# Statistics of the edge messages: one instruction for two tiles, no aggregation, the sum of a small constant on GpSimd

## The chip, the core and the metric

The kernel runs on one core of one Trainium2 chip. The metric is the device time of one execution in microseconds (us). A core has TensorE (PE in the profile, with its weight loads as PEld), VectorE (DVE), ScalarE (ACT), GpSimd (POOL) and SyncE (SP). Each works through its own list of instructions in order; semaphores tie the lists together. An operation that a semaphore makes wait also holds everything behind it on the same engine.

## What is computed

One layer of a graph network over 3125 nodes of 256 features and 50000 edges, followed by a linear attention and a mixture of experts. The change is in the part that works on edges, cut here to that part:

```python
hi, hj = h[ei], h[ej]
msg = silu(concat(hi, hj, d2) @ mW1 + mb1)            # one row of 256 values an edge
mu  = mean(msg); var = mean(square(msg - mu))         # over the 256 values
msg = (msg - mu) * rsqrt(var + 1e-5) * ln_g + ln_b
msg = silu(msg @ mW2 + mb2)
agg = segment_sum(msg, ei)
```

## The kernel before

The edges are sorted by target node and cut into 224 units of 256 edges. A unit is two tiles (`G = 2`) of 128 edges, one edge a partition. The units run through a pipeline written out by hand: in step `n` each engine works on several units at different stages, in a fixed order. Ten steps make a turn (`TURN = 10`), because ten buffers are used in rotation; the first two turns and the tail are written out, and the turns between are a hardware loop.

What each engine does in step `n`:

- GpSimd works in pairs of units. `roots` waits for the variances of a pair (`spread_ok`) and computes 1/sqrt of four values a partition by a power of -0.5 (`nw_y`, L739). Then `gather` issues four indirect DMAs (L752), two for each of the two units that lie six units ahead, which bring rows of `dst_table` into `msg1`. Before two of the five pairs of a turn, `stage` copies the next gather indices (L747). All of this is one list in order.
- TensorE turns the normalised messages (`msg1n`, unit n-6, L832), multiplies unit n-7 by the second weight in three partial products (L1044, L1045, L1049), picks the source rows of unit n (L1061) and sums the messages of unit n-8 into their node rows (L1071).
- VectorE makes the one-hot rows of unit n+1 (L1700), on odd steps adds epsilon to the variances of a pair (`nw_v`, L1705), on even steps waits for GpSimd's root of the pair n-4 and forms the shift `1 - mean * root` of it (`nw_b`, L1712 and L1726), adds the node sums of unit n-9 (L1723), makes the low part of the split of unit n-6 (`msg1T_lo`, L1731), takes the statistics of both tiles of unit n-1 (L1738, twice), adds the picked and gathered rows of unit n (L1743), makes another one-hot (L1750), and aggregates the statistics of each tile into mean and variance (`emv`, L1755, twice).
- ScalarE evacuates the turned messages (L1331), normalises unit n-5 with `nw_y` as scale and `nw_b` as shift (L1338), and applies silu twice (L1345, L1350).

The number one in the shift carries the bias: the prepared second weight `w2c` has column sums that equal the bias of the product, so that a one added to every normalised value adds it. The statistics instruction gives six numbers for its input: count, mean and sum of squared deviations of the elements at even places, and the same of those at odd places. The aggregation merges these into one mean and one variance.

`roots` of pair m needs the variances of units m and m+1. VectorE waits for its result near the start of step m+4, ahead of L1723, L1731, L1738 and L1743 of that step.

## Time and profile before

| | us |
|---|---|
| device time, median of 3 runs | 1673.52 (1671.7 to 1680.5) |
| span of the profiled execution, first to last instruction | 1439.5 |
| median of the runs less that span | 234.0 |
| TensorE, VectorE, ScalarE, GpSimd busy, of the span | 1279.5, 1182.8, 932.1, 878.1 |
| edge pipeline, start of the first and of the last VectorE addition L1743 | 339.0 and 1052.4 |

The profiled execution's own device time is not recorded, only its span; the lowest and the median of the three timed runs are 0.1% apart. The edge pipeline is half of the span. A group row of the profile gives source line, engine, operation, tiles written and read, shapes and count, then busy time and the mean of one instruction. A row of the timeline gives the start, the time it took, the instruction, and in brackets the idle time of its engine before it and what ended it.

### The profile page before, as it was taken

To read this page: it belongs to the slowest core of one execution; us is meant where nothing else is said; L and a number is where in the kernel's file an instruction comes from. 1 tells how busy PE (TensorE), PEld (TensorE's weight loads), DVE (VectorE), ACT (ScalarE), POOL (GpSimd) and SP (SyncE) were. 2 spreads that over 40 slices of the span, in tenths; PEclk is the share of its full clock that TensorE was granted. 3 is DMA by queue.
4 is the path that set the end of the run, shared out by engine and by line. 5 is a ranking of instruction groups with operands and counts; after the bars stand their busy time and mean duration, and the time that the engine had idled before them with its cause. 6 is when DMAs were issued, how large, how long until landed. Compare 5 with 4: busy or idle time off the path is not lost.

```text
span 1439.5 us, 32698 instructions
## 1 busy us (share of the span) xinstructions
PE 1279.5 (89%) x8927; PEld 1149.6 (80%) x8928; DVE 1182.8 (82%) x3550; ACT 932.1 (65%) x1856; POOL 878.1 (61%) x885
## 2 busy tenths in 40 slices
PE   2678899996999999999999999999998847999990
PEld 1366778786999999999999999999886635988890
DVE  6999778726999999999999999999954688666662
ACT  0877444414778887888878888888753544666660
POOL 2188774035887778787777787878710014767761
PEclk7599999997999999999999999999999978999995
DMA  3911100022333333333333333336860162444447
GB/s 118 197 34 43 31 13 23 1 68 64 111 104 98 104 106 101 101 99 112 99 101 102 107 103 101 100 108 93 86 193 0 43 253 72 75 73 73 73 60 280
DMA packets 71387, 133.94 MB, mean 93 GB/s; under 512 B 23126, under 2 KB 43868, under 8 KB 70695
## 3 DMA queue, kind: packets, MB, share of 16 engines
q0 software_dynamic: 36560, 77.33, 24.1%
q1 hardware_dynamic: 33986, 52.62, 12.0%
q10 hardware_dynamic: 780, 3.24, 0.6%
q8 instruction: 31, 0.51, 0.2%
q14 instruction: 30, 0.25, 0.1%
HBM read 107.71 MB, written 25.29 MB: 92 GB/s over the span
## 4 chain that ended last, share of the span: by engine, by line
PE 71%; DVE 17%; DMA 4%; issue 3%; ACT 2%; POOL 1%; DVEq 0%; ACTq 0%; POOLq 0%; SPq 0%
PE ps L1071 12%; PE ps L832 9%; PE ps L1045 7%; PE ps L1049 7%; PE ps L1044 7%; PE ps L1061 7%; DVE place_val_t L1579 3%; DVE lane_hot_e_t L1574 2%; PE ps L1170 2%; PE ps L1201 2%; PE ps L1199 2%; PE ps L1200 2%; PE ps L1172 2%; PE ps L1171 2%; PE ps L1102 2%
## 5 line engine op out<-in xcount | busy, mean ns | idle before, releaser
L752 POOL DMA_INDIRECT msg_t<-dst_table,stage_idx x448 | 444.2, 991 | 128.7 <-issue 126.5
L1044 PE MATMUL ps<-w_hi_t,msg1T_hi_t 128*128 128x256 f32 x896 | 252.4, 303 | 0.0
L1338 ACT ACTIVATE msg1n_t<-msg_t,nw_b,nw_y 128x256 f32<-128x256 f32 x448 | 242.4, 590 | 0.0
L1350 ACT ACTIVATE msg_t<-msg_t 128x512 f32<-128x512 f32 x224 | 141.6, 632 | 149.4 <-DVE msg_t L1743 148.8
L1045 PE MATMUL ps<-w_lo_t,msg1T_hi_t 128*128 128x256 f32 x896 | 234.2, 283 | 0.0
L1071 PE MATMUL ps<-msg_t,hot_t 128*125 128x256 f32 x896 | 230.4, 379 | 0.2 <-issue 0.2
L1049 PE MATMUL ps<-w_hi_t,msg1T_lo_t 128*128 128x256 f32 x896 | 179.8, 282 | 0.0
L1045 PEld LDWEIGHTS ps<-w_lo_t,msg1T_hi_t 128*128 128x128 f32 x896 | 171.9, 192 | 0.0
L1044 PEld LDWEIGHTS ps<-w_hi_t,msg1T_hi_t 128*128 128x128 f32 x896 | 170.3, 190 | 0.0
L1738 DVE BATCH_NORM_STATS2 est<-msg_t 128x6 f32<-128x256 f32 x448 | 166.2, 413 | 1.2 <-ACT msg_t L1350 1.2
L1071 PEld LDWEIGHTS ps<-msg_t,hot_t 128*125 128x125 f32 x896 | 152.0, 187 | 14.2 <-issue 0.4
L1731 DVE TENSOR_TENSOR msg1T_lo_t<-ps,msg1T_hi_t 128x512 fp32r<-128x512 f32 x224 | 154.0, 688 | 2.7 <-ACT msg1T_hi_t L1331 2.5
L1743 DVE TENSOR_TENSOR msg_t<-ps,msg_t 128x512 f32<-128x512 f32 x224 | 151.2, 675 | 3.6 <-DMA msg_t<-dst_table,stage_idx 2.3
L721 POOL DMA_INDIRECT sorted_edges<-sort_sb_t,chunk_to x112 | 130.9, 1168 | 36.8 <-issue 33.8
L1049 PEld LDWEIGHTS ps<-w_hi_t,msg1T_lo_t 128*128 128x128 f32 x896 | 139.5, 191 | 0.0
L739 POOL TENSOR_TENSOR nw_y<-nw_v,minus_half 128x4 f32<-128x4 f32 x112 | 116.8, 1043 | 36.8 <-DVE nw_v L1705 29.6
L832 PE MATMUL ps<-ident,msg1n_t 128*128 128x128 f32 x896 | 135.7, 274 | 3.7 <-ACT msg1n_t L1338 3.7
L832 PEld LDWEIGHTS ps<-ident,msg1n_t 128*128 128x128 f32 x896 | 111.1, 140 | 29.1 <-ACT msg1n_t L1338 6.5
L1331 ACT ACTIVATE msg1T_hi_t<-ps 128x512 fp32r<-128x512 f32 x224 | 130.9, 584 | 3.5 <-PE ps L832 3.0
L1345 ACT ACTIVATE msg_t<-ps 128x512 f32<-128x512 f32 x224 | 129.9, 580 | 2.6 <-PE ps L1049 2.5
L1061 PE MATMUL ps<-src_hi_t,hotT_t 127*128 x448 | 120.0, 288 | 8.7 <-DVE hotT_t L1700 8.7
L1061 PE MATMUL ps<-src_lo_t,hotT_t 127*128 x448 | 119.5, 288 | 0.0
(374 smaller groups left out, 3081.1 us busy)
## 6 DMA issues: line engine op xcount, KB each, us to landing
near_rows<-row_list SPq DMA_DIRECT2D x44, 320.0 KB
w_sb_t<-in_L_ffn_W_dram SPq DMA_DIRECT2D x16, 512.0 KB, 8.5
msg_t<-dst_table,stage_idx POOLq DMA_INDIRECT x448, 2.8
res_t<-in_x_dram SPq DMA_DIRECT2D x1, 3125.0 KB
total<-zero_chunks_t SPq DMA_DIRECT2D x1, 3125.0 KB, 26.8
dst_table<-dst_stage SPq DMA_DIRECT2D x25, 125.0 KB
xm_table<-xm_t POOLq DMA_DIRECT2D x5, 625.0 KB, 7.5
sum_a_t<-total SPq DMA_DIRECT2D x5, 625.0 KB, 10.6
```

Source lines behind the costliest of these rows:

```text
L752: pool.indirect_dma_start(out=msg1[:, k, j, :], out_offset=None, in_=dst_table, in_offset=bass.IndirectOffsetOnAxis(stage_idx[:, G * k + j ...
L832: return pe.transpose(out_, in_, ident[0:rows, 0:rows])
L1044: pe.matmul(o[j], part(msg1T_hi, j, c), w2_hi[:, c, :], start=(c == 0), stop=False)
L1045: pe.matmul(o[j], part(msg1T_hi, j, c), w2_lo[:, c, :], start=False, stop=False)
L1049: m = pe.matmul(o[j], part(msg1T_lo, j, c), w2_hi[:, c, :], start=False, stop=(c == KD - 1))
L1061: m = pe.matmul(bank(1 + k % 2, D, first=j * D), hotT[0:HR, k, j * 128:j * 128 + 128], table[0:HR, bass.ts(blk[k], 1), :].rearrange("p a n ...
L1071: m = pe.matmul(bank(7 * (kl % 2), D, rows=NP), hot[:, kl % 2, j, 0:NP], msg2[:, kl % 2, j, :], start=(j == 0), stop=(j == G - 1))
L1338: m = A(msg1n[:, (kl + 1) % 2, j, :], msg1[:, kk, j, :], ACT.Identity, bias=nw_b[:, kk, j:j + 1], scale=nw_y[:, kk, j:j + 1])
L1350: A(v, v, ACT.Silu).then_inc(msg1_sb, 1)
L1731: dve.tensor_tensor(msg1T_lo[:, k % 2], bank(3 + k % 2), msg1T_hi[:, k % 2].bitcast(F32), ALU.subtract)\
L1738: st.did(dve.bn_stats(est[:, kk, j, :], msg1[:, kk, j, :]))
L1743: dve.tensor_tensor(v, bank(1 + k % 2), v, ALU.add).then_inc(pre_sb, 1)
```

## The change

- The two statistics instructions a unit become one over 512 elements. It reads the two tiles interleaved (`p j n -> p n j`), so that the elements at even places are tile 0 and those at odd places tile 1. Its six results are count, mean and sum of squared deviations of each tile.
- The aggregations (two a unit) are gone, and the buffer `emv` with them. The sum of squared deviations is 256 times the variance, so the root is now of `256 * var + 256 * eps`, which is the old root divided by 16. The second weight is multiplied by 16 instead, once, ahead of the pipeline.
- Epsilon is no longer added on VectorE (L1705 before) but on GpSimd: `roots` first adds `eps_sum` to the four sums, waits for that addition through a semaphore, and then takes the power. The statistics instruction itself now releases `spread_ok`, once a unit.
- The added one (divided by 16) is no longer added to the shift on VectorE (L1726 before) but in ScalarE's evacuation of the turned messages, as a bias, and in VectorE's low part, which becomes an operation with two arithmetic steps.

```diff
@@ roots, on GpSimd
-                pool.wait_ge(spread_ok, m // 2 + 1 if isinstance(m, int) else pairs + k // 2 + 1)
+                pool.wait_ge(spread_ok, m + 2)
                 if not isinstance(free, int) or free > 0:
                     pool.wait_ge(msg1n_sb, free)
+                st.did(pool.tensor_tensor(nw_v[:], est[:, k:k + 2, :, 2], eps_sum[:].rearrange("p (a b) -> p a b", b=G), ALU.add))
+                st.join()
                 pool.tensor_tensor(nw_y[:, k:k + 2, :], nw_v[:], minus_half[:].rearrange("p (a b) -> p a b", b=G),
                                    ALU.pow).then_inc(pow_ok, 1)
@@ edge_step, on ScalarE
-                    A(msg1T_hi[:, kl % 2], bank(3 + kl % 2), ACT.Copy).then_inc(msg1T_sb, 1)
+                    A(msg1T_hi[:, kl % 2], bank(3 + kl % 2), ACT.Copy, bias=1.0 / ROOT_D).then_inc(msg1T_sb, 1)
@@ edge_step, on VectorE
-                if k % 2 and here(n - 3, UNITS):
-                    slot = (k - 3) % TURN
-                    st.join()
-                    dve.tensor_scalar(nw_v[:], emv[:, slot:slot + 2, :, 1], EPS, None, ALU.add).then_inc(spread_ok, 1)
...
-                    nw.did(dve.scalar_tensor_tensor(shifts, emv[:, slot:slot + 2, :, 0], -1.0, nw_y[:, slot:slot + 2, :],
-                                                    ALU.mult, ALU.mult))
+                    dve.scalar_tensor_tensor(shifts, est[:, slot:slot + 2, :, 1], -1.0, nw_y[:, slot:slot + 2, :],
+                                             ALU.mult, ALU.mult).then_inc(rstd_ok, 1)
...
-                if pair_on:
-                    nw.join()
-                    dve.tensor_scalar(shifts, shifts, 1.0, None, ALU.add).then_inc(rstd_ok, 1)
...
-                    dve.tensor_tensor(msg1T_lo[:, k % 2], bank(3 + k % 2), msg1T_hi[:, k % 2].bitcast(F32), ALU.subtract)\
-                       .then_inc(msg1T_lo_sb, 1)
+                    dve.scalar_tensor_tensor(msg1T_lo[:, k % 2], bank(3 + k % 2), 1.0 / ROOT_D, msg1T_hi[:, k % 2].bitcast(F32),
+                                             ALU.add, ALU.subtract).then_inc(msg1T_lo_sb, 1)
...
-                    for j in range(G):
-                        st.did(dve.bn_stats(est[:, kk, j, :], msg1[:, kk, j, :]))
+                    dve.bn_stats(est_pairs[:, kk, :], msg1[:, kk].rearrange("p j n -> p n j")).then_inc(spread_ok, 1)
...
-                if here(m_, UNITS):
-                    for j in range(G):
-                        st.did(dve.bn_aggr(emv[:, kk, j, :], est[:, kk, j, :]))
@@ before the pipeline
-            step(dve.tensor_copy(w2_hi[:], w2c[:]))
-            dve.tensor_tensor(w2_lo[:], w2c[:], w2_hi[:].bitcast(F32), ALU.subtract).then_inc(w_lo_ok, 1)
+            step(dve.tensor_scalar(w2_hi[:], w2c[:], ROOT_D, None, ALU.mult))
+            dve.scalar_tensor_tensor(w2_lo[:], w2c[:], ROOT_D, w2_hi[:].bitcast(F32), ALU.mult, ALU.subtract).then_inc(w_lo_ok, 1)
```

How the instructions stand on GpSimd inside the hardware loop, in the kernel before: one pair without new indices, then one with them (`stage_idx`). The four gathers of a pair are one row; the rows named ISA and REGISTER_ALU are register work of the sequencer.

```order
L739 TENSOR_TENSOR nw_y<-nw_v,minus_half 128x4 [waits msg1n_sb,spread_ok]
L752 DMA msg_t<-dst_table,stage_idx 128x256 x4
L480 ISA
L747 ISA [waits row_in2,row_in3,row_in1,row_in0]
L747 COPY stage_idx<-recs_t 128x8
L33 ISA
L736 REGISTER_ALU [waits pool_step]
L738 REGISTER_ALU [waits spread_ok]
L739 TENSOR_TENSOR nw_y<-nw_v,minus_half 128x4 [waits msg1n_sb]
```

The same place on GpSimd in the changed kernel, from the addition of one pair to the power of the next.

```order
L743 TENSOR_TENSOR nw_v<-est,eps_sum 128x4 [waits msg1n_sb,spread_ok]
L33 REGISTER_ALU
L745 TENSOR_TENSOR nw_y<-nw_v,minus_half 128x4 [waits pool_step]
L758 DMA msg_t<-dst_table,stage_idx 128x256 x4
L483 ISA
L753 ISA [waits row_in2,row_in3,row_in1,row_in0]
L753 COPY stage_idx<-recs_t 128x8
L33 REGISTER_ALU
L740 REGISTER_ALU [waits pool_step]
L743 TENSOR_TENSOR nw_v<-est,eps_sum 128x4 [waits msg1n_sb,spread_ok]
L33 REGISTER_ALU
L745 TENSOR_TENSOR nw_y<-nw_v,minus_half 128x4 [waits pool_step]
```

Each pair has one more operation on GpSimd (L743), and the power now waits for it by `pool_step`. The gathers stand behind both.

On VectorE in the loop, the kernel before, from the node sums of an even step to its aggregations:

```order
L1723 TENSOR_TENSOR agg_t<-agg_t,ps 125x256
L33 REGISTER_ALU
L1726 TENSOR_SCALAR nw_b<-nw_b 128x4 [waits newton_step]
L1731 TENSOR_TENSOR msg1T_lo_t<-ps,msg1T_hi_t 128x512 [waits msg2_ps,msg1T_sb]
L1738 BN_STATS est<-msg_t 128x6 [waits msg1_sb]
L1738 BN_STATS est<-msg_t 128x6
L1740 REGISTER_ALU
L1743 TENSOR_TENSOR msg_t<-ps,msg_t 128x512 [waits row_in8,pre_ps]
L33 REGISTER_ALU
L1750 ISA [waits sum_ps,dve_step]
L1750 TENSOR_TENSOR hot_t<-iota,recs_t 128x2x125
L1755 BN_AGGR emv<-est 128x2 x2
```

And the same stretch of an even step in the changed kernel:

```order
L1721 TENSOR_TENSOR agg_t<-agg_t,ps 125x256
L1726 SCALAR_TENSOR_TENSOR msg1T_lo_t<-ps,msg1T_hi_t 128x512 [waits msg2_ps,msg1T_sb]
L1732 BN_STATS est<-msg_t 128x6 [waits msg1_sb]
L1737 TENSOR_TENSOR msg_t<-ps,msg_t 128x512 [waits row_in2,pre_ps]
L1742 TENSOR_TENSOR hot_t<-iota,recs_t 128x2x125 [waits sum_ps]
```

Four instructions of an even step are gone there, and two waits of VectorE on itself (`newton_step`, `dve_step`); what is left stands in the same order.

## Rows read from the trace of the kernel before

**Rows 1.** Busy us of each engine in one stretch of the loop (PE, PEld, DVE, ACT, POOL)

```profile
500.00:600.00 100.00, 100.00 (x750) 94.83 (x749) 97.49 (x327) 80.90 (x157) 79.03 (x85) 1.00 0.35 103
```

**Rows 2.** Chain that ended last, 700 to 725 us: start, us, what

```profile
700.74 0.44 PE ps L832 x4
...
723.24 0.44 PE ps L832 x4
```

**Rows 3.** Timeline of VectorE in the loop; the last row opens a turn

```profile
699.62 0.74 DVE L1738 BATCH_NORM_STATS2 est<-msg_t 128x6 f32<-128x256 f32 x2
700.28 0.67 DVE L1743 TENSOR_TENSOR msg_t<-ps,msg_t 128x512 f32<-128x512 f32 x1
...
701.20 0.24 DVE L1755 BATCH_NORM_AGGREGATE emv<-est 128x2 f32<-128x6 f32 x2
701.36 0.32 DVE L1700 TENSOR_SCALAR hotT_t<-near_rows,row_col 125x256 fp32r<-125x256 f16 x1
701.59 0.16 DVE L1705 TENSOR_SCALAR nw_v<-emv 128x4 f32<-128x4 f32 x1
701.81 0.42 DVE L1723 TENSOR_TENSOR agg_t<-agg_t,ps 125x256 f32 x1
...
702.75 0.74 DVE L1738 BATCH_NORM_STATS2 est<-msg_t 128x6 f32<-128x256 f32 x2
...
718.17 0.42 DVE L1723 TENSOR_TENSOR agg_t<-agg_t,ps 125x256 f32 x1 [0.71 <-issue]
```

**Rows 4.** Timeline of GpSimd, one turn: each power, and what precedes two

```profile
702.12 1.05 POOL L739 TENSOR_TENSOR nw_y<-nw_v,minus_half 128x4 f32<-128x4 f32 x1
703.35 1.00 POOL L752 DMA_INDIRECT msg_t<-dst_table,stage_idx  x1 [0.18 <-issue]
...
708.36 0.20 POOL L747 CAST stage_idx<-recs_t 128x8 int32 x1
708.80 1.03 POOL L739 TENSOR_TENSOR nw_y<-nw_v,minus_half 128x4 f32<-128x4 f32 x1 [0.24 <-POOL stage_idx L747]
...
714.86 1.05 POOL L739 TENSOR_TENSOR nw_y<-nw_v,minus_half 128x4 f32<-128x4 f32 x1
...
721.48 1.04 POOL L739 TENSOR_TENSOR nw_y<-nw_v,minus_half 128x4 f32<-128x4 f32 x1 [0.40 <-DVE nw_v L1705]
...
727.89 1.04 POOL L739 TENSOR_TENSOR nw_y<-nw_v,minus_half 128x4 f32<-128x4 f32 x1 [0.37 <-DVE nw_v L1705]
...
734.28 1.05 POOL L739 TENSOR_TENSOR nw_y<-nw_v,minus_half 128x4 f32<-128x4 f32 x1
```

**Rows 5.** Groups of GpSimd by shape, whole span

```profile
L801 POOL TENSOR_TENSOR rstd<-rstd,minus_half 125x4 f32<-125x4 f32 x6 | 6.1, 1010 | 79.7 <-DVE rstd L1799 79.7
L714 POOL TENSOR_TENSOR mw_lo_t<-mw_sb,mw_hi_t 128x1024 fp32r<-128x1024 f32 x1 | 2.5, 2465 | 4.7 <-ACT mw_hi_t L1256 4.7
L715 POOL TENSOR_TENSOR bw_cut<-bw,bw_cut 4x256 fp32r<-4x256 f32 x1 | 1.0, 1004 | 0.0
L747 POOL CAST stage_idx<-recs_t 128x8 int32<-128x8 f32 x4 | 0.8, 195 | 0.0
L801 POOL TENSOR_TENSOR rstd<-rstd,minus_half 125x1 f32<-125x1 f32 x1 | 0.6, 580 | 0.0
L731 POOL MEMSET minus_half<- 128x4 f32 x1 | 0.1, 102 | 59.8 <-issue 59.8
```

**Rows 6.** Timeline of GpSimd, written-out turns: a power that waits for GpSimd's own copy

```profile
356.54 0.20 POOL L747 CAST stage_idx<-recs_t 128x8 int32<-128x8 f32 x1
356.82 1.13 POOL L739 TENSOR_TENSOR nw_y<-nw_v,minus_half 128x4 f32<-128x4 f32 x1
```

**Rows 7.** Group of the gathers, 500 to 1000 us

```profile
L752 POOL DMA_INDIRECT msg_t<-dst_table,stage_idx x312 | 310.2, 994 | 89.1 <-issue 88.2 <-DVE nw_v L1705 0.6 <-ACT msg1n_t L1338 0.3
```

**Rows 8.** Timeline of VectorE, start of the pipeline

```profile
351.60 0.16 DVE L1712 SCALAR_TENSOR_TENSOR nw_b<-emv,nw_y 128x4 f32<-128x4 f32 x1 [1.27 <-POOL nw_y L739]
```

**Rows 9.** Group of VectorE by shape, whole span

```profile
L1683 DVE SCALAR_TENSOR_TENSOR mixG_lo_t<-ps,mixG_hi 128x256 fp32r<-128x256 f32 x2 | 0.8, 424 | 6.2 <-ACT mixG_hi L1315 6.2
```

24 lines of the change are left out of this document (9 added, 15 removed).

## The prediction

> **What bounds the kernel now.** I read the busy time by stretches first. In a 100 us stretch of the edge pipeline TensorE is busy for all of it, its weight loads for 94.8, VectorE for 97.5, ScalarE for 80.9 and GpSimd for 79.0 [rows 1]. Three engines could be the bound by these figures: TensorE and VectorE by their shares, and GpSimd because its share leaves out the gaps between its DMA instructions. So I went to the chain that ended last. Between 700 and 725 us it runs through TensorE alone. The turned messages (L832) come at 700.74 and, seven units later, at 723.24 [rows 2]: 22.50 / 7 = 3.214 us a unit, 32.14 us a turn of ten, without a stop. TensorE is the bound, and its list is untouched by the change.
>
> VectorE is the next. One step of it runs from 699.62 to 702.75 [rows 3], 3.13 us, ten of them 31.3, and once a turn it sits idle for 0.71 us on register work before L1723 (the last row of [rows 3]). Together 32.0 of the 32.14: it has next to nothing to spare, but it doesn't pace TensorE, whose interval stays even across that stop.
>
> GpSimd is the third, and the one that matters here. Its powers (L739) start at 702.12 and, five pairs later, at 734.28 [rows 4]: 32.16 us a turn, as it must be. In that turn it waited for VectorE twice. The wait of 0.40 us at 721.48 stands behind a copy of indices, where 0.24 us pass in any case (the row at 708.80), so 0.16 of it is spare; the 0.37 us at 727.89 stand behind a gather, where rows without a wait show no gap, so about 0.35 is spare. Without the two the turn would take 32.16 - 0.51 = 31.65 us. GpSimd has 32.14 - 31.65 = **0.49 us to spare in a turn**, 0.10 us a pair. Its 79% of busy time hides this, because the gathers take 994 ns each but stand 0.3 us apart for no wait (88.2 us of "issue" before 312 of them) [rows 7]. At the start of the pipeline GpSimd is even late: VectorE waits 1.27 us for the power of the second pair [rows 8].
>
> **What the change does, part by part.**
>
> *VectorE, statistics.* Two instructions of 256 elements take 0.66 us from their start to that of L1743 [rows 3]. One of 512 elements doesn't occur before; the nearest row is L1743 itself with 512 elements, 0.67 us and 0.08 less to the next start, so about 0.6. Its interleaved read (neighbours 1 KB apart) has no row. Lower bound 0.6, upper bound half speed, 1.2. I take 0.6.
>
> *VectorE, the rest.* The two aggregations take 0.16 us of a step (701.20 to 701.36), L1705 takes 0.22 of every second step (701.59 to 701.81) [rows 3], L1726 is of the same kind. That is 0.06 + 0.16 + 0.11 + about 0.1 = 0.43 us less a step: 2.7 instead of 3.13, and 27.7 a turn instead of 32.0. None of it shortens TensorE's 32.14. Off the bound, this part is worth nothing in the loop. Where the pipeline fills and drains, VectorE's steps are on the path for some four or five units; I put 1 us there (bounds 0 and 3).
>
> *VectorE and ScalarE, the moved one.* The low part gets a second arithmetic step. The only such instruction that reads PSUM takes 424 ns for 256 elements [rows 9], against 0.42 us for the plain L1723 of that size [rows 3]. No cost. ScalarE's evacuation gets a constant bias; should it cost a little, ScalarE has 19 us of 100 idle to cover it [rows 1]. The scaled weight is made once.
>
> *VectorE, its waits on itself.* Two go. The wait for the power stays where it was.
>
> *GpSimd, the addition.* Each pair now has an addition of 128x4 ahead of the power, and the power waits for it through a semaphore. That wait has a row: in the written-out turns a copy of indices ends at 356.54 + 0.20 = 356.74, and the power that waits for it starts at 356.82 [rows 6], **0.09 us**. The addition itself has none; this is the price on which the whole result hangs. Its bounds: the cheapest instruction of that shape is the memset, 0.10 us; a copy with one input takes 0.20; a power of a single element, which has two inputs and certainly more work, takes 0.58 [rows 5]. Within these, the two-input rows say more. The powers of four and of one element take 1010 and 580 ns [rows 5], 143 ns an element and 437 ns that don't depend on the number. The subtractions of 1024 and of 256 elements take 2465 and 1004 ns [rows 5]: 1.9 ns an element and 517 ns fixed. Two different operations agree that a two-input instruction on GpSimd costs 0.44 to 0.52 us before its first element. I take **0.44 us**, since the power's pair of rows has the addition's own shape and partitions. An addition then costs 0.44 + 0.09 = 0.53 us a pair, 2.65 a turn.
>
> The Trainium skill (GPSIMD Engine Reference, section 3.1) gives another account: about 2.6 cycles an element for a two-input addition at 1.2 GHz, and 4497 ns measured for 2048 elements. By these, 2048 elements take 4437 ns, 60 ns are left, and four elements would cost about 0.07 us; the estimate for the kernel would be 1676.5. The row of 1024 elements speaks against so small a rest: at that rate it would leave 246 ns, and the row of 256 would leave 449. The same page (section 4.1) names VectorE, not GpSimd, for elementwise work, which bears on this change.
>
> *Nothing is taken from GpSimd.* Its five powers, twenty gathers and two copies a turn stay. The variances reach it earlier, since the statistics release it directly: about 701.75 - 700.30 = 1.45 us sooner [rows 3]. That moves its list once, not each turn.
>
> **The sum.** GpSimd's turn becomes 31.65 + 2.65 = 34.30 us, against TensorE's 32.14: 2.16 us more a turn. Gathers go with 109 pairs, 108 intervals, 21.6 turns: 46.7 us. Against that stand the 1.45 us of earlier variances, some 1.3 us by which the last powers are ahead of need today (the power at 702.12 ends at 703.17, well before the even step of VectorE that uses it), and 1 us of fill and drain: 3.7. The result is 1673.5 + 46.7 - 3.7 = **1716.5 us**, 2.6% slower. The profile has no device time of its own execution, so I add the difference to the median; what lies outside the span, 234 us, is left alone.
>
> **What is late next.** When GpSimd is the bound, VectorE stands at the shift of an even step and waits for the power. Behind it stand the node sums, the low part (for which TensorE's third product waits), the statistics and the addition that ScalarE's silu waits for. So all engines fall to GpSimd's pace. The shorter VectorE step can't win it back, because power and gathers are one list. The gathers themselves stay early: they are issued at most 6.9 us after their power for units six and seven steps ahead.
>
> **The rivals.**
>
> *Short addition* (0.15 to 0.35 us, like the one-input copy). At 0.20 the turn gains 5 x 0.29 - 0.49 = 0.96 us, in 21.6 turns 20.7, less 3.7: 1690.5. For it: all one-input rows of GpSimd are that cheap. Against it: both two-input pairs.
>
> *Hidden addition, no change.* At the memset's 0.10 us: 5 x 0.19 - 0.49 = 0.46, 9.9 less 3.7, 1679.7; below that it falls to 1674. This is also where the change doesn't do what it says for time: VectorE was never the bound. It needs an addition under about 0.12 us. The page's account above belongs here.
>
> *Slow statistics.* If the interleaved read runs at half speed, a VectorE step is 2.7 + 0.6 = 3.3 and a turn 33.7 us, 1.6 above TensorE's: 35 us, 1708 if GpSimd isn't slower still. From 1.05 us for the statistics on, VectorE would bind. Against it: nothing in the trace reads so, either way.
>
> *Faster.* If TensorE's 3.214 us a unit were VectorE's pace in disguise (the two differ by 0.4%), and the addition cost nothing, the turn could fall to GpSimd's 31.65: 0.49 x 21.6 = 10.6 us, with the fill 1 more, 1662. It needs both; the even interval of TensorE across VectorE's stop speaks against the first and every row of GpSimd against the second.
>
> **How the numbers follow.** A measurement tells a change of this kernel from none at about 0.5%, 8.4 us. Forecast (addition 0.35 to 0.55 us, 1707 to 1728): 0.55. Short addition (1685 to 1707): 0.22. Slow statistics: 0.05. Hidden: 0.14, nearly all within 0.5%. Faster: 0.04. Together slower 0.83, same 0.13, faster 0.04. The range leaves out the hidden and the faster case and the power's 0.58 us (1731): 1684 to 1730.
>
> **What would show it.** Right: GpSimd's powers 34.3 us apart a turn with no wait for VectorE before the addition; an addition of about 0.44 us with 0.09 behind it; waits of VectorE's shift for the power, near 2 us a turn; VectorE busy for about 80% of the loop instead of 97.5, TensorE for about 94%; a statistics instruction of about 0.68 us. Wrong: TensorE still at 3.214 us a unit with GpSimd waiting (a short addition), or waits of TensorE for VectorE with the statistics above 1 us. The forecast would also miss if the gathers changed from their 994 ns, twenty a turn: 0.03 us each is 0.6 a turn, 13 us in all.

## The result, and the profile after

The changed kernel takes **1569.65 us** (median of 4 runs, 1567.6 to 1572.4) against 1672.61 (4 runs, 1670.9 to 1680.5) for the kernel before on the same chip: a ratio of **0.9388** (95% interval 0.9356 to 0.9419), 103 us or 6.1% faster. I had forecast 1716.5, slower, and had given a gain a chance of 0.04. The sign and the size are wrong.

One thing must be said first, or the numbers don't fit: the execution whose profile I read for the prediction (span 1439.5) is unlike all the timed ones. In each of the 15 other profiles here the device time is the span plus 1.7 to 2.2 us (changed kernel: span 1570.6, device time 1572.4 in the same execution). The kernel before, profiled again, has a span of 1692.8. And the kernel before itself took 1670 to 1674 us (median) in some sets of runs and 1696 to 1698 in others, both on one and the same chip, for a reason that no run shows: ratios from different sets of runs can't be compared more closely than 1.5%.

So the rows after stand here beside the new profile of the kernel before too. The columns are those of [rows 1]. The kernel before, profiled again:

```profile
500.00:600.00 100.00, 83.32 (x588) 73.92 (x587) 77.48 (x257) 64.39 (x123) 61.73 (x67) 1.00 0.27 79
```

The changed kernel:

```profile
500.00:600.00 100.00, 94.83 (x686) 85.85 (x686) 83.61 (x189) 75.89 (x145) 75.19 (x92) 1.00 0.34 95
```

In [rows 1] TensorE was busy for all of the 100 us. In a typical execution of the kernel before it is idle for a sixth of it, at the full granted clock (1.00, its level of 2.4 GHz), and the change takes most of that idle time away. The pipeline (start of the first to the last addition of gathered rows) takes 713.4 us in the profile read for the prediction, 886.5 in the new one, 764.6 in the changed kernel. (The new one was taken in a slower set of runs, so its pipeline may be up to 25 us longer than in the set of the result.) What comes behind it takes 385 to 387 us in all three. What comes ahead takes 339, 421 and 421.

GpSimd's groups in the changed kernel, by shape, over the span (they answer to [rows 4] and [rows 5]):

```profile
L758 POOL DMA_INDIRECT msg_t<-dst_table,stage_idx x448 | 445.0, 993 | 127.9 <-issue 125.2 <-ACT msg1n_t L1341 1.5 <-DVE est L1732 0.3
L745 POOL TENSOR_TENSOR nw_y<-nw_v,minus_half 128x4 f32<-128x4 f32 x112 | 117.3, 1048 | 8.8
L743 POOL TENSOR_TENSOR nw_v<-est,eps_sum 128x4 f32<-128x4 f32 x112 | 22.7, 203 | 57.1 <-DVE est L1732 34.7 <-ACT msg1n_t L1341 12.6 <-POOL stage_idx L753 5.3
```

The addition takes 203 ns, not the 440 I took. VectorE's and ScalarE's changed instructions, from the page of the changed kernel:

```profile
L1732 DVE BATCH_NORM_STATS2 est<-msg_t 128x6 f32<-128x512 f32 x224 | 155.7, 695 | 2.1 <-ACT msg_t L1353 2.1
L1726 DVE SCALAR_TENSOR_TENSOR msg1T_lo_t<-ps,msg1T_hi_t 128x512 fp32r<-128x512 f32 x224 | 155.0, 692 | 57.0 <-ACT msg1T_hi_t L1334 43.5
L1334 ACT ACTIVATE msg1T_hi_t<-ps 128x512 fp32r<-128x512 f32 x224 | 130.4, 582 | 8.6 <-PE ps L835 6.8
```

One statistics instruction with the interleaved read takes 695 ns, no longer than the two that it replaces (0.74 us in [rows 3]); what 512 elements in an unbroken row would take, no run shows. The second arithmetic step costs nothing (692 ns, against 688 for L1731 in the kernel before profiled again), and neither does the bias. There the evacuation took:

```profile
L1331 ACT ACTIVATE msg1T_hi_t<-ps 128x512 fp32r<-128x512 f32 x224 | 130.4, 582 | 11.4 <-remote 7.1 <-PE ps L832 4.1
```

**Where the kernel before loses its time.** Its waits in the new profile, 600 to 1100 us (engine and line, what it waited for, us in total, times, longest):

```profile
ACT msg_t L1350 <- DVE msg_t L1743: 133.7, 111, 2.9
POOL nw_y L739 <- DVE nw_v L1705: 119.1, 58, 2.6
DVE msg_t L1743 <- remote: 73.6, 49, 2.3
```

The timeline of its VectorE, one of those waits:

```profile
697.41 0.74 DVE L1738 BATCH_NORM_STATS2 est<-msg_t 128x6 f32<-128x256 f32 x2
699.63 0.69 DVE L1743 TENSOR_TENSOR msg_t<-ps,msg_t 128x512 f32<-128x512 f32 x1 [1.49 <-remote]
700.24 0.41 DVE L1750 TENSOR_TENSOR hot_t<-iota,recs_t 128x250 f32<-128x250 f32 x1
...
700.96 0.16 DVE L1705 TENSOR_SCALAR nw_v<-emv 128x4 f32<-128x4 f32 x1
```

and of its GpSimd beside it:

```profile
693.37 1.04 POOL L739 TENSOR_TENSOR nw_y<-nw_v,minus_half 128x4 f32<-128x4 f32 x1 [2.58 <-DVE nw_v L1705]
694.60 1.02 POOL L752 DMA_INDIRECT msg_t<-dst_table,stage_idx  x1 [0.19 <-issue]
695.93 0.97 POOL L752 DMA_INDIRECT msg_t<-dst_table,stage_idx  x1 [0.30 <-issue]
697.21 0.95 POOL L752 DMA_INDIRECT msg_t<-dst_table,stage_idx  x1 [0.30 <-issue]
698.46 0.95 POOL L752 DMA_INDIRECT msg_t<-dst_table,stage_idx  x1 [0.31 <-issue]
701.30 1.04 POOL L739 TENSOR_TENSOR nw_y<-nw_v,minus_half 128x4 f32<-128x4 f32 x1 [1.90 <-DVE nw_v L1705]
```

L1743 waits for two things: the gathered rows, and TensorE's pick of the source rows (`pre_ps`). "Remote" names neither. The trace also holds the time at which each semaphore rose. The packets of this unit's rows had ended by 690.0, 9.6 us before (the burst of packets behind its two gathers, which are issued at 685.81 and 687.11). TensorE's matmul for it has its modelled end at 697.15, but **its signal rose at 699.61**, and L1743 started 0.02 us later. The signals of TensorE around it, all in order (from the trace's semaphore records; my own listing):

```
raised by           modelled end   signal rose
second product      696.67         697.40
pick of rows (L1061) 697.15        699.61
node sums           698.01         700.35
turned messages     698.45         700.41
second product      699.89         700.53
pick of rows        700.36         700.59
```

Four signals that were due over 2.35 us (698.01 to 700.36) rise within 0.24 us (700.35 to 700.59): they had been held. It is the same for every wait of L1743: it waits longer than 0.15 us 60 times from 500 to 1000 us, and all 60 times it starts within 0.13 us of the rise of `pre_ps`. So none of these waits is for gathered rows. The signals of VectorE, ScalarE and GpSimd rise within 0.01 us of the end of their instructions in every kernel here, in the same 500 us.

The Trainium skill (Perfetto Trace Analysis, section on the Tensor Engine Instruction) says that the reported end of a matmul is an estimate and that the signal is pushed later, when PSUM has acknowledged the writes; the trace agrees that the signal can come behind the reported end, with 0.01 us between the two in the profile read for the prediction and up to 3.14 us in the new one. Whether PSUM's acknowledgement is what comes late, no run here shows.

The same listing for all of TensorE's signals from 500 to 1000 us, with the time of a pair of units (matched to the last matmul that raises the semaphore, so the lateness is rather understated):

```
kernel                          signals  over 0.3 us late  90%    max   us a pair
before, read for the prediction   623        0.00          0.01   0.01    6.43
before, profiled again            491        0.59          2.37   3.14    8.14
changed                           528        0.46          1.60   2.84    6.92
```

And the changed kernel, the same 528 signals, by when a signal was due, counted from the start of the first of the four gathers that GpSimd issues for a pair (starts at 0, 1.33, 2.60, 3.92, end of the last 4.87):

```
due at        signals   held over 0.3 us   rose at (median)
0.0 to 2.5      211          0.03          on time
2.5 to 3.5       33          0.45          mixed
3.5 to 4.0       44          0.95          5.70
4.0 to 4.5       70          1.00          5.76
4.5 to 5.0       38          1.00          5.82
5.0 to 5.5       64          1.00          5.84
5.5 to 6.0       50          0.24          5.90
6.0 and on       18          0.00          on time
```

**TensorE's signals are held while GpSimd issues the later ones of a row of gathers, and most rise together 0.8 to 1.0 us after the last issue.** In the kernel before the hold sets in earlier: signals due in the first 1.5 us behind the start of the row come on time (60 of 61), those due from 2.0 us on are held (59 of the 61 due from 2.0 to 2.5). There this closes a loop over one pair: power 693.37, four gathers to 699.41, signal 699.61 (an early one, 0.2 us behind the last issue), L1743 699.63, L1705 700.96, next power 701.30: 7.9 us for two units, 3.97 a unit, against TensorE's own 3.214. The loop has two parts that the change touches: that GpSimd waits for something behind L1743 at all, and the 1.67 us from the start of L1743 to that of the power, in which stand the aggregations and L1705.

GpSimd in the changed kernel:

```profile
685.28 0.20 POOL L743 TENSOR_TENSOR nw_v<-est,eps_sum 128x4 f32<-128x4 f32 x1 [0.59 <-ACT msg1n_t L1341]
685.55 1.05 POOL L745 TENSOR_TENSOR nw_y<-nw_v,minus_half 128x4 f32<-128x4 f32 x1
...
690.88 0.95 POOL L758 DMA_INDIRECT msg_t<-dst_table,stage_idx  x1 [0.30 <-issue]
691.83 0.21 POOL L753 CAST stage_idx<-recs_t 128x12 int32 x1
692.15 0.20 POOL L743 TENSOR_TENSOR nw_v<-est,eps_sum 128x4 f32<-128x4 f32 x1
```

and its VectorE:

```profile
691.31 0.69 DVE L1732 BATCH_NORM_STATS2 est<-msg_t 128x6 f32<-128x512 f32 x1
692.81 0.69 DVE L1737 TENSOR_TENSOR msg_t<-ps,msg_t 128x512 f32<-128x512 f32 x1 [0.81 <-remote]
```

The held addition (now L1737) is still late by 0.81 us at 692.81, but GpSimd's next pair began at 692.15 without it: the addition of epsilon waits for the statistics instruction of the unit before, which stands ahead of L1737 in VectorE's list. In this pair the hold is no longer in GpSimd's loop. Over all pairs GpSimd still waits for VectorE now and then, but a tenth as long as the 119.1 us above, in the same stretch of 600 to 1100 us:

```profile
POOL nw_v L743 <- DVE est L1732: 12.4, 30, 1.4
```

### The profile page after: what moved, and what is told of

It is laid out like the page before. It is cut to its first block, busy times and chain, and to the rows that moved or that the text cites. A ratio compares the mean times of both kernels' runs of the same rounds, so it can differ in the third digit from the quotient of the medians.

```text
span 1570.6 us, 31395 instructions
## 1 busy us (share of the span) xinstructions
PE 1313.9 (84%) x8927; PEld 1153.2 (73%) x8928; DVE 1134.9 (72%) x2654; ACT 940.1 (60%) x1856; POOL 896.4 (57%) x998
## 4 chain that ended last, share of the span: by engine, by line
PE 46%; DVE 21%; ACT 12%; issue 10%; another core or an unknown queue 7%; DMA 3%; ACTq 1%; DVEq 1%; POOLq 0%; SPq 0%
PE ps L835 7%; PE ps L1064 6%; ACT msg1n_t L1341 5%; DVE msg_t L1737 5%; ACT msg1T_hi_t L1334 4%; DVE place_val_t L1582 3%; PE ps L1052 3%; PE ps L1048 3%; PE ps L1047 3%; PE ps L1074 2%; DVE lane_hot_e_t L1577 2%; PE ps L1173 2%; DVE est L1732 2%; PE ps L1202 2%
## 5 line engine op out<-in xcount | busy, mean ns | idle before, releaser
L1737 DVE TENSOR_TENSOR msg_t<-ps,msg_t 128x512 f32<-128x512 f32 x224 | 152.8, 682 | 63.8 <-remote 36.6
L1726 DVE SCALAR_TENSOR_TENSOR msg1T_lo_t<-ps,msg1T_hi_t 128x512 fp32r<-128x512 f32 x224 | 155.0, 692 | 57.0 <-ACT msg1T_hi_t L1334 43.5
L835 PE MATMUL ps<-ident,msg1n_t 128*128 128x128 f32 x896 | 141.2, 280 | 32.5 <-ACT msg1n_t L1341 31.0
L835 PEld LDWEIGHTS ps<-ident,msg1n_t 128*128 128x128 f32 x896 | 102.6, 141 | 86.6 <-ACT msg1n_t L1341 56.9
L1732 DVE BATCH_NORM_STATS2 est<-msg_t 128x6 f32<-128x512 f32 x224 | 155.7, 695 | 2.1 <-ACT msg_t L1353 2.1
L724 POOL DMA_INDIRECT sorted_edges<-sort_sb_t,chunk_to x112 | 126.7, 1131 | 36.8 <-issue 33.8
```

What stands on the lines that cost most here:

```text
L835: return pe.transpose(out_, in_, ident[0:rows, 0:rows])
L1726: dve.scalar_tensor_tensor(msg1T_lo[:, k % 2], bank(3 + k % 2), 1.0 / ROOT_D, msg1T_hi[:, k % 2].bitcast(F32), ALU.add, ALU.subtract).then ...
L1732: dve.bn_stats(est_pairs[:, kk, :], msg1[:, kk].rearrange("p j n -> p n j")).then_inc(spread_ok, 1)
L1737: dve.tensor_tensor(v, bank(1 + k % 2), v, ALU.add).then_inc(pre_sb, 1)
```

## The experiments

Times are ratios to the kernel before in the same set of runs. Where two kernels were timed in different sets, their own times in us stand beside.

### The kernel before once more

The file of the kernel before, unchanged.

> This is the kernel before, unchanged, with a new profile. Theory A (the profile that the prediction was made from was taken in an execution that is not like the timed ones): the new profiled execution has a span near its device time, about 1670 us, and the 230 us more than in the old profile lie in waits that the old one doesn't show, mostly in the edge pipeline (more than 3.6 us a unit instead of 3.214). Theory B (the device time holds 234 us around the span, for every execution): the span is again near 1440 us with a device time near 1672. The rival to A inside the span: the extra time lies outside the edge pipeline, in which case the pipeline again takes 713 us.

Measured: 1693.97 us, ratio 0.9974 (0.9948 to 0.9999), span of the profiled execution 1692.8. That is theory A: the device time is the span plus 1.7 us, and the profile read for the prediction was of another kind of execution. Its rival, that the time lies outside the pipeline, holds for a third: 82 of the 253 us lie ahead of it.

### First theory: the gathers are asked for too late

The first thing I thought was that the gathered rows arrive late, since "remote" can be a transfer, and that the loop runs from a power through gathers issued behind it to the addition that needs them, over four units before and six after. Four runs went on this.

**Release as late as before, in the changed kernel:**

```diff
                 pool.wait_ge(spread_ok, m + 2)
+                pool.wait_ge(pre_sb, min(m + 3, UNITS) if isinstance(m, int) else m + 3)
```

> The changed kernel with one wait more and no work more: GpSimd's addition and power for a pair m, m+1 also wait until VectorE has done its addition for unit m+2 (the operation that waits for the gathered rows), which is the point from which the kernel before let them go. Theory (release): the gain came from the earlier release, since the gathers for units m+6 and m+7 stand behind the power of pair m on GpSimd, and so the path from that power through the gathers and VectorE's addition back to a power closes over 4 units here and over 6 in the changed kernel. Its length was 16.7 us in the repeat of the kernel before (power of unit 66 at 684.6, power of unit 70 at 701.3); about 0.9 us of it (the variance step on VectorE and its waits) stays away, so 15.8 / 4 = 3.95 us a unit against 3.475 in the changed kernel and 4.08 before: some 100 us over 217 units, that is 0.98 of the kernel before (0.965 to 1.0). Rival (instructions): the gain came from the six instructions fewer a pair on VectorE and their waits on its own results; then this wait costs little and the time stays at 0.94 (0.93 to 0.95).

Measured: 0.9593 (0.9553 to 0.9633). This misses both ranges. The wait alone gives back a third of the gain, with no work added, so the release is a cause; but not at the 0.98 that a loop over four units would give. Nor does it restore the old loop: where GpSimd waits for the addition, it goes on 0.78 us after the addition's start (median of 25 waits over 0.5 us, 600 to 1100 us), against 1.66 in the kernel before (58 waits), since the aggregations and L1705 no longer stand between. GpSimd's powers are 6.9 us apart in the median and 8.3 in the slowest twentieth: the longer loop closes only for some pairs. It waits for the named line:

```profile
POOL nw_v L744 <- DVE msg_t L1738: 43.6, 33, 1.8
DVE msg_t L1738 <- remote: 37.7, 26, 1.7
```

**Release as early as after, in the kernel before**, with all of its instructions kept:

```diff
                         st.did(dve.bn_stats(est[:, kk, j, :], msg1[:, kk, j, :]))
+                    st.join()
+                    dve.memset(carrier[:, 0:1], 0.0)
+                    for j in range(G):
+                        st.did(dve.bn_aggr(emv[:, kk, j, :], est[:, kk, j, :]))
+                if k % 2 == 0 and here(n - 2, UNITS):
+                    slot = (k - 2) % TURN
+                    st.join()
+                    dve.tensor_scalar(nw_v[:], emv[:, slot:slot + 2, :, 1], EPS, None, ALU.add).then_inc(spread_ok, 1)
                 if here(n, UNITS):
                     dve.wait_ge(pre_ps, n + 1)
```

(the later aggregation and L1705 are taken out).

> The kernel before, with all of its instructions, but the aggregation and the epsilon step moved ahead of the addition that waits for the gathered rows, so that GpSimd is let go one step earlier (one 128x1 fill a unit more on VectorE carries a wait). Release: the loop closes over 6 units as in the changed kernel, with about 1.2 us more in it for the two aggregations and the epsilon step, 0.2 us a unit: 3.65 us a unit, some 90 us less than before, 0.95 of it (0.935 to 0.97). Instructions: VectorE does a little more than before, so 1.0 to 1.02.

Measured: 0.9667 (0.9634 to 0.97), inside the range expected for the release and far from the 1.0 to 1.02 for the instructions. The order alone gives more than half of the gain, though VectorE now has more to do than before (91.6 of 100 us):

```profile
500.00:600.00 100.00, 94.29 (x660) 81.67 (x660) 91.56 (x313) 72.13 (x137) 69.78 (x75) 1.00 0.31 88
```

**Gathers ahead of the power**, in both kernels:

```diff
-                roots(m, k, ahead + 2 - TURN)
+                free = ahead + 2 - TURN
+                if not isinstance(free, int) or free > 0:
+                    pool.wait_ge(msg1n_sb, free)
+                    pool.tensor_tensor(carrier[:, k:k + 1], minus_half[:, 0:1], minus_half[:, 1:2], ALU.add)
                 for q in range(2):
                     if here(ahead + q, UNITS):
                         gather((slot + q) % TURN)
+                roots(m, k)
```

> The kernel before with GpSimd's order turned round: the gathers for units m+6 and m+7 are issued ahead of the power of pair m, which now only stands behind them; one 128x1 addition a pair on GpSimd carries the wait for the free buffers. Release: the gathers stand behind the power of pair m-2 alone, so the loop closes over 6 units with 16.7 us in it, 2.8 us a unit, which is below what the engines need; the next limit is TensorE's 3.2 to 3.4 us a unit: 0.90 to 0.95 of the kernel before. Rival (rate of transfers: the rows arrive late because the queues or the memory are slow, whenever they are asked for): 1.0.

Measured: 0.9942 (0.9918 to 0.9965).

> The changed kernel with the same turned order on GpSimd. Release: the loop closes over 8 units, well under the engines' own time; from 3.475 us a unit to TensorE's 3.2 to 3.4, or GpSimd's, whose turn of ten units has 32.16 us of work in the kernel before plus 5 x 0.28 for the addition plus 5 x 0.25 for the carrying one = 34.8, 3.48 a unit: so no more than 0.93 of the kernel before, 0.925 to 0.945, about the changed kernel's own time. Rival (late transfers whatever the order): 0.94 to 0.95.

Measured: 0.9805 (0.9777 to 0.9832): 4% slower than the changed kernel. Both miss. The power behind four gathers is late for VectorE. In the first of the two:

```profile
POOL carrier L765 <- ACT msg1n_t L1341: 90.2, 64, 1.8
...
DVE nw_b L1715 <- POOL nw_y L738: 48.0, 60, 1.5
```

GpSimd's list now waits for buffers to come free before it can compute the roots that free them, a loop of my own making. So these two runs don't decide about late rows: the addition's own "remote" waits did fall (14.9 us in place of 73.6, 600 to 1100 us), and others came in their place. They sent me back to the semaphore records and the held signals told above; what rules late rows out are those records, in which all 60 waits of L1743 end with TensorE's signal.

### What the parts are worth

**The added one alone, in the kernel before** (ScalarE's evacuation with `bias=1.0`, VectorE's low part with `1.0, ..., ALU.add, ALU.subtract`, L1726 taken out).

> The kernel before with one part of the change alone: the added one in the two evacuations (as 1.0, the weights unscaled) and not in VectorE's small step on the shifts, so one instruction and one wait on its own result fewer a pair on VectorE. Theory (loop): before, one pair of units takes 8.1 us because a loop closes over it: GpSimd's power (1.04), its four gathers, the hold of TensorE's completion signals that ends 0.9 us after the last gather, VectorE's addition for the even unit (0.69), the epsilon step, and the next power. The step that is left out is not in this loop: 0.99 to 1.0 of the kernel before. Rival (VectorE's work): 0.25 us fewer a pair on VectorE, 112 pairs, 28 us, 0.983.

Measured: 0.9917 (0.9888 to 0.9946). Inside the 0.99 to 1.0 of the loop theory, at the end with the larger gain: 0.8%, by the interval 0.5 to 1.1%, so the step is worth a little although it isn't in the loop.

**Epsilon back on VectorE, in the changed kernel:**

```diff
+                if k % 2 == 0 and here(n - 2, UNITS):
+                    slot = (k - 2) % TURN
+                    st.join()
+                    dve.tensor_scalar(nw_v[:], est[:, slot:slot + 2, :, 2], D * EPS, None, ALU.add).then_inc(spread_ok, 1)
```

> The changed kernel with the epsilon addition back on VectorE, straight behind the statistics instruction and still ahead of the addition that waits for the rows. Theory (GpSimd is the bound of the changed kernel: its power of a pair starts 6.93 us after that of the pair before, and it waits little): GpSimd loses 0.27 us a pair, 112 pairs, 30 us of 1570; VectorE gains 0.16 and a wait on its own result, and has room: 0.92 to 0.93 of the kernel before, against 0.939 for the changed one. Rival (TensorE is the bound at 96% busy): no change, 0.935 to 0.945. That VectorE's wait for itself costs the rest a third possibility: 0.945 to 0.955.

Measured: 0.9361 (0.9333 to 0.939). Not the 0.92 to 0.93 of the theory that GpSimd is the bound; it lies in the range of the rival.

**The addition on GpSimd made twice, in the changed kernel:**

```diff
+                st.did(pool.tensor_tensor(nw_x[:], est[:, k:k + 2, :, 2], eps_sum[:].rearrange(...), ALU.add))
+                st.join()
                 st.did(pool.tensor_tensor(nw_v[:], est[:, k:k + 2, :, 2], eps_sum[:].rearrange(...), ALU.add))
```

> The changed kernel with GpSimd's epsilon addition made twice, the second behind the first: 0.27 us more a pair on GpSimd and nothing else. GpSimd as the bound: 112 x 0.27 = 30 us more, 0.957 of the kernel before (0.95 to 0.965). TensorE as the bound: 0.94 to 0.945. My prediction had priced the addition at 0.53 us with its wait; by that 0.974.

Measured: 0.9462 (0.9432 to 0.9493). One addition less is worth 0.3% or nothing, one more costs 0.7%: about 12 us, 0.11 us a pair of the 0.27 that it takes. It lies under the range of GpSimd as the bound (0.95 to 0.965) and at the edge of that of TensorE. So GpSimd alone is not the bound of the changed kernel, and TensorE, which has its own 6.43 us in a pair of 6.92, isn't quite either. That GpSimd's work shifts the hold, and all of them set the pace together, is my reading, and no run shows it by itself.

### What holds TensorE's signals

**An eighth of the bytes, in the kernel before:** the gathers of all units behind the first ten fetch 32 columns (`out=msg1[:, k, j, 0:32]`, from the table seen as rows of 32).

> The kernel before with the gathers of all units behind the first ten fetching 32 of a row's 256 numbers (128 bytes in place of 1024; the other columns keep older rows, so the output is another one): the same number of gathers and descriptors, an eighth of the bytes. It tells what holds TensorE's completion signals in the kernel before (up to 2.9 us, once a pair, until 0.9 us after the last gather is issued). If the rows that land hold them, the hold goes, the loop shortens by some 2 us a pair, and the next limit is GpSimd's own 6.4 to 6.9 us a pair in place of 8.1: 0.89 to 0.93 of the kernel before. If the issue of the gathers on GpSimd holds them, or something else: 0.98 to 1.0, and the signals come as late as before.

Measured: 1.0052 (1.0031 to 1.0073), with 25 GB/s moved in place of 79, and 0.58 of TensorE's signals over 0.3 us late (0.59 before). The number of bytes doesn't hold them. The number of transfers is the same here.

```profile
500.00:600.00 100.00, 85.46 (x596) 76.53 (x596) 78.30 (x260) 64.88 (x124) 62.72 (x68) 0.98 0.12 25
```

**No gathers, in the kernel before:**

```diff
-            def gather(k):
+            def gather(k, whole):
                 for j in range(G):
+                    if not whole:
+                        continue
                     pool.indirect_dma_start(
```

with VectorE's wait for the rows of the first turn kept for all.

> The kernel before with the gathers of all units behind the first ten left out (VectorE adds to what stands in the buffers, so the output is another one); everything else is issued as before. It tells whether TensorE's completion signals are held by the gathers at all. If they are, all signals come within 0.1 us of the matmul's modelled end, VectorE no longer waits ahead of its addition for even units, and the kernel runs at the pace of TensorE's own work, 3.2 us a unit in place of 4.07: some 190 us less, 0.88 to 0.90 of the kernel before. If the hold is TensorE's own (its completions come late at full load whatever GpSimd does), signals still come 1.5 to 2.9 us late and the pace stays over 3.5 us a unit: 0.93 or more.

Measured: **0.8964** (0.892 to 0.9008), 1518.69 us.

```profile
500.00:600.00 100.00, 100.00 (x750) 94.88 (x749) 97.06 (x328) 80.75 (x156) 16.99 (x22) 1.00 0.06 20
```

This is [rows 1] again, GpSimd apart: 750 matmuls in 100 us, 6.43 us a pair, no signal more than 0.02 us late.

**A power in the place of each gather** (as above, with `pool.tensor_tensor(spare[:, k, j], ones[:, 0:4], minus_half[:], ALU.pow)` where it says `continue`).

> As the run before, but with a small power of 128x4 numbers (1.04 us in the kernel before, a gather's issue 0.98) in the place of each gather that is left out: GpSimd is about as busy as before (5 x 1.1 = 5.6 us a pair against 6.3), and issues no transfers. If time on GpSimd is what closes the loop, signals come on time and the pace is set by GpSimd and the path through VectorE: the loop of a pair without the hold is 5.6 + 0.3 for the signal and VectorE's addition, well under TensorE's 6.4, so 0.88 to 0.91, near the run without gathers. If it isn't the gathers but any busy GpSimd that holds the signals, they come late here and not in the run before: 0.95 or more.

Measured: 0.8962 (0.8921 to 0.9004), 1517.48 us. GpSimd is as busy as in the profile read for the prediction, and nothing is held:

```profile
500.00:600.00 100.00, 100.00 (x750) 94.88 (x749) 97.10 (x327) 80.73 (x157) 77.93 (x86) 1.00 0.06 20
```

So it is the indirect transfers, not GpSimd's time and not the bytes. Their issue and their way through the DMA queues are taken away together here, and no run parts them. What the traces show is when the hold ends: in the kernel before, the last packets of a pair end 1.5 us behind the last issue, and the held signals rise 1.0 us behind it, 0.6 us before (medians of 61 pairs, 500 to 1000 us). With an eighth of the bytes the packets end at 1.1 us and the signals rise at 0.85. They don't wait for the data to have landed; that is why I speak of the issue.

**No gathers, in the changed kernel.**

> The changed kernel with the gathers of all units behind the first ten left out, as was done to the kernel before (the output is another one). If the change gains only by taking the held signals out of GpSimd's loop, there is nothing to gain here: TensorE's 3.21 us a unit bounds both, and the time is that of the kernel before without gathers, 0.896 of the kernel before (0.89 to 0.90). If VectorE's lighter step is worth something by itself (0.44 us a unit by its rows), up to 0.44 x 214 = 94 us less: 0.84.

Measured: 0.8969 (0.892 to 0.9018), 1517.65 us. Without the gathers, and so without the hold, the change gains nothing: the two kernels are equal within the measurement (0.8964 and 0.8969), though VectorE's busy time falls from 97.1 to 90.2 of 100 us:

```profile
500.00:600.00 100.00, 100.00 (x749) 94.75 (x748) 90.24 (x204) 81.54 (x156) 19.88 (x37) 1.00 0.07 20
```

### Breaking the rows of transfers

**The power between the gathers of the two units, in the changed kernel:**

```diff
                     if here(ahead + q, UNITS):
                         gather((slot + q) % TURN)
+                    if q == 0:
+                        power(k)
```

> The changed kernel with GpSimd's power of a pair put between the gathers of unit m+6 and those of unit m+7 (the addition stays ahead of both), so that no four gathers stand in an unbroken row: 1.05 us lie in one break and 0.27 in the other. In the changed kernel signals that fall due in the first 2 us behind the start of a row of four come on time and all later ones are held until 0.9 us after its end, up to 2.8 us. If the hold grows with an unbroken row, it is cut to some 1 us here, and the pace comes down towards GpSimd's own 6.6 to 6.7 us a pair: 0.92 to 0.935 of the kernel before. If it is made by the last gather alone whatever stands ahead, the held time stays and there is one hold more a pair, and the power comes 2.5 us later, which is within the 3.4 us that VectorE leaves it: 0.94 to 0.97.

Measured: **0.9212** (0.9188 to 0.9237), 1560.34 us, with not one instruction taken away. The ratio is 1.9% below that of the changed kernel, but the kernel before was a slower one here (1696.5 us, against 1672.6). In their own times the gain is 0.6% (1560.34 against 1569.65), and the pipeline takes 751.9 us in place of 764.6. 0.36 of the signals are over 0.3 us late, against 0.46.

```profile
686.66 0.20 POOL L743 TENSOR_TENSOR nw_v<-est,eps_sum 128x4 f32<-128x4 f32 x1 [1.10 <-DVE est L1736]
687.30 0.99 POOL L760 DMA_INDIRECT msg_t<-dst_table,stage_idx  x1 [0.45 <-issue]
688.59 0.96 POOL L760 DMA_INDIRECT msg_t<-dst_table,stage_idx  x1 [0.30 <-issue]
689.57 1.04 POOL L747 TENSOR_TENSOR nw_y<-nw_v,minus_half 128x4 f32<-128x4 f32 x1
690.80 1.02 POOL L760 DMA_INDIRECT msg_t<-dst_table,stage_idx  x1 [0.19 <-issue]
```

The number lies in the range expected for a hold that grows with the row, but the hold isn't cut to 1 us: single signals are still up to 2.7 us late. It is cut in two. The held signals rise in two bunches, most at 3.0 to 3.4 us (99 of 190) and at 6.2 to 6.6 us (65) from the start of the pair's first gather, so behind the second gather and behind the fourth (my listing, 500 to 1000 us). The edit also moves two gathers ahead of the power; moving all four ahead made the changed kernel slower (0.9805), so it is not that alone.

**A power after every second scatter, ahead of the pipeline, besides:**

```diff
                         in_=sort_sb[:, g, j].rearrange("p c f -> p (c f)"), in_offset=None).then_inc(scattered, 16)
+                    if (RUNS * g + j) % 2:
+                        st.join()
+                        st.did(pool.tensor_tensor(pause[:], ones[:, 0:4], ones[:, 0:4], ALU.pow))
```

> The kernel of the run before (power between the gathers) with one more edit, ahead of the edge pipeline: GpSimd makes a small power of 128x4 numbers after every second one of its 112 scatters of sorted edges, which stood in an unbroken row from 71 to 231 us. It adds work (56 x 1.1 = 62 us on GpSimd, which waits 137 us behind the scatters anyway) and takes none away. In the kernel before, TensorE is busy 17.6 and 14.0 of 50 us from 150 to 250 us, and it was 42 and 48 in the profile read for the prediction, and some of its signals come 12 to 16 us late there. If the unbroken row of scatters holds them, most of the 82 us come back: 1480 to 1510 us, 0.87 to 0.89 of the kernel before. If the loss has another cause (loads, clock), no gain or a small loss: 0.92 to 0.93.

Measured: **0.8948** (0.8915 to 0.8982), 1496.61 us. The stretches from 150 to 250 us, of the kernel of the run before, which lacks the pauses alone (the kernel before, profiled again, has 17.59 and 14.04 us of TensorE there):

```profile
150.00:200.00 50.00, 16.33 (x129) 14.07 (x129) 12.63 (x34) 5.54 (x14) 38.15 (x39) 0.67 0.09 19
200.00:250.00 50.00, 14.18 (x75) 12.86 (x76) 7.77 (x17) 6.88 (x17) 23.78 (x25) 0.55 0.02 4
```

and of this kernel:

```profile
150.00:200.00 50.00, 42.58 (x327) 37.53 (x325) 37.48 (x90) 22.60 (x52) 43.69 (x37) 1.00 0.11 25
200.00:250.00 50.00, 48.24 (x262) 41.02 (x261) 41.48 (x96) 22.73 (x39) 42.85 (x43) 1.00 0.03 4
```

There too a row of indirect transfers had held TensorE's signals, and with them TensorE, VectorE and ScalarE: from 100 to 250 us 0.45 of the signals are over 0.3 us late and the worst 13.5 us in the kernel of the run before, 0.09 and 1.3 us here (my listing). The pipeline now begins at 363 us in place of 419, 56 us sooner, though 56 powers of work were added; 82 us was what the profile read for the prediction had promised. In their own times the gain on the run before is 63.7 us (1560.34 less 1496.61), 56 of them ahead of the pipeline. The time lies in the 1480 to 1510 us that I expected; the ratio is a little above the 0.87 to 0.89, because the kernel before was the faster one in this set (1670.6 us). What isn't told apart: the powers break the row, and they also spread it, 112 scatters over 71 to 295 us in place of 71 to 231. The granted clock in these stretches was 0.67 and 0.55 with TensorE busy for 16 and 14 of 50 us, and is 1.00 here with 43 and 48.

## Why the prediction was wrong, point by point

**The first step: what bounds the kernel.** "TensorE is the bound" and the chain that "runs through TensorE alone", 3.214 us a unit, are true of the execution in [rows 1] and [rows 2]. Of the timed ones none took under 1664 us. There (the second profile) a pair takes 8.1 us in a loop of GpSimd's power, its gathers, the held signal, L1743 and L1705. The step that failed is this one, that TensorE bounds the kernel. What let it through is the sentence "what lies outside the span, 234 us, is left alone": a span 232 us below the lowest run was the sign that the profile and the runs were not of the same kind. Between that span and the one of the second profile, 1692.8, lie 253 us: 173 in the pipeline (886.5 - 713.4) and 82 ahead of it. (In the set of that second profile the kernel before took 1698.3 us, 25 more than in the set from which I forecast.)

**"The variances reach it earlier ... That moves its list once, not each turn."** This is the step that hid the gain, valued once at 1.45 us. In a loop that closes through VectorE's L1743 it counts for every pair. The early release alone gave 3.3 of the 6.1 per cent, the late release took 2.1 of them away, and without gathers (no hold) the change gains 0.0 (0.8969 against 0.8964). It isn't the whole gain: with the late release 4.1% are left. By the rows, much of it can lie in VectorE's work between L1743 and the power (1.66 us before, 0.78 with the late release), which the prediction had put at nothing as "off the bound". No run takes away that work alone, so the split stays open.

**GpSimd's addition, 0.44 us.** Measured 0.203, and 0.28 from its start to that of the power (median; the wait of 0.09 us from [rows 6] was nearly right, here 0.07). It lies at the price of the one-input copy in [rows 5], the 0.20 of my rival *short addition*. The fixed parts that I took from the two pairs of two-input rows are not those of an addition of 128x4; one of the pairs isn't even of one form, since its row of 256 elements works on 4 partitions and its row of 1024 on 128. The figures of the Trainium skill (GPSIMD Engine Reference, section 3.1), by which I had estimated 0.07, are too low by 0.13: neither the page's rate nor my rows gave this one. This error did not make the sign: with 0.28 us the sum was 31.65 + 1.4 = 33.05 us a turn, 19.7 us more less 3.7, 1689.5, still slower. What one such addition costs here the doubled one shows, 12 us.

**GpSimd's turn, 34.30 us.** The pair takes 6.92 us in the changed kernel, 34.6 a turn. This agrees, but not for the reason given: GpSimd's work is 33.05 by the measured price, and the rest are waits. It is luck.

**TensorE busy 94%, VectorE 80%, statistics 0.68 us, no cost of the second arithmetic step and the bias:** measured 94.8 and 83.6 of 100 us, 0.695, and none. The prices held. The two busy shares came near by the same luck as GpSimd's turn, since they follow from a pace near 34.3 us. The waits of VectorE's shift for the power, near 2 us a turn, didn't come (L1710 waits 1.0 us in the whole span).

**The rivals.** *Slow statistics* fell with 0.695 us. *Short addition* had the price right and still came out slower than the kernel before, because it shares the step above. *Faster* had the right sign, at 0.04, with another mechanism and a ninth of the size. None of the rivals had a signal that comes later than its matmul; in the profile read for the prediction there was none, all of its 623 signals rose 0.01 us after the modelled end.

Settled by runs: that TensorE's signals are held by the indirect transfers (with, with few bytes, without, with powers instead), that the change gains nothing where they are absent, and that both kernels are at 3.21 us a unit without them. Not settled: by which path in the chip the signals are held, whether the issue or the later handling of the transfers does it, why the kernel before comes in two speeds, and why the execution read for the prediction, the same program with all its gathers and scatters, shows no hold at all.

## What to carry to other kernels

Before a profile is read, put its span beside the timed runs. Here they lay 2 us apart in fifteen profiles and 234 us apart in the one that misled me, whose waits were not those of the timed kernel. Where a consumer of TensorE starts well after the matmul's modelled end, look at when the semaphore rose: what is on the path then is the signal, and it pays to move it out of any loop (let the next engine go from an instruction ahead of it). Indirect transfers from GpSimd are best not issued in long rows beside a busy TensorE: a small instruction of another kind between them made the pipeline 12.7 us shorter in one place, and in another the part ahead of it 56 us shorter. The version with both takes 1496.61 us, 0.8948 of the kernel before.

## What the runs showed of the hardware that I had not expected

- TensorE's completion signals rose up to 3.1 us after the modelled end of their matmuls while GpSimd issued four indirect transfers in a row. In the changed kernel those due in the first 2.5 us came on time and the later ones together, 0.8 to 1.0 us after the last issue; in the kernel before the hold set in after some 2 us. The signals of VectorE, ScalarE and GpSimd were never more than 0.01 us late beside them. In one execution of the kernel before, with all of its transfers, there was no hold at all.
- With an eighth of the bytes the hold was the same (1.0052 of the time); with powers of the same length in the place of the transfers it was gone (0.8962).
- In an unbroken row of scatters ScalarE waited up to 16.4 us at a time for TensorE's results (L1283, four waits of 12.2 to 16.4 us from 179 to 238 us), and TensorE's granted clock was 0.65 and 0.53 in the stretches in which it was busy for 18 and 14 of 50 us.
- A statistics instruction over two interleaved tiles (512 elements, neighbours 1 KB apart) takes 695 ns, two over 256 elements 413 each. An addition of 128x4 on GpSimd takes 203 ns, a power of the same shape 1048.
